# Attention on one core: one transpose per group of maxima, the way through DRAM, and two steps moved between engines

## The reference

```
x = x + alpha * attention(gamma * rmsnorm(x) + beta)
rmsnorm(x) = x * rsqrt(mean(x * x) + 1e-6)
attention: 16 heads of width 16;
  softmax(0.25 * q k^T) v over 512 keys, then @ W_o^T
```

## Time and profile before

| | us |
|---|---|
| median of 3 runs | 1261.8 |
| lowest, highest | 1261.4, 1264.4 |
| the profiled execution's own time | 1264.4 |
| its span, first to last instruction | 1262.6 |

### The profile page before, as it was taken

One profiled execution on the slowest core, in us unless ns is written; L12 is line 12 of the kernel. 1 busy time (PEld: TensorE's weight loads), 2 busy tenths in 40 slices (PEclk: granted clock), 3 DMA queues, 4 the chain that ended last, 5 costly groups with the idle time before them and its releaser, 6 DMA issues. The chain is left out here.

```text
span 1262.6 us, 16655 instructions
## 1 busy us (share of the span) xinstructions
PE 1096.2 (87%) x5282; PEld 654.8 (52%) x5282; DVE 777.3 (62%) x1318; ACT 674.9 (53%) x882; POOL 143.0 (11%) x173
## 2 busy tenths in 40 slices
PE   4879999993578999999999998988828999999994
PEld 3657777772334334343434343432217777777772
DVE  3756776666167777778776878767016555555453
ACT  4453333332306667777777777666424355554445
POOL 0000000001212122232323223021100000000000
PEclk8889999996657999999999999989658999999997
DMA  9522222240342344353435353521030000000000
GB/s 313 224 76 76 76 75 75 76 113 0 120 81 102 84 135 102 95 139 89 131 75 147 64 172 64 169 64 28 12 122 1 2 17 17 17 13 4 17 17 33
DMA packets 54047, 102.09 MB, mean 81 GB/s; under 512 B 8560, under 2 KB 19312, under 8 KB 52976
## 3 DMA queue, kind: packets, MB, share of 16 engines
q1 hardware_dynamic: 51104, 98.86, 27.0%
q10 hardware_dynamic: 2896, 2.64, 0.9%
HBM read 65.02 MB, written 31.72 MB: 77 GB/s over the span
## 5 line engine op out<-in xcount | busy, mean ns | idle before, releaser
L1056 DVE TENSOR_REDUCE mx<-mx_ps 128x1 f32<-128x512 f32 x512 | 329.9, 683 | 129.8 <-PE mx_ps L1131 129.5
L1131 PE MATMUL mx_ps<-kring,qring 48*128 48x512 f32 x512 | 220.1, 490 | 29.5 <-DVE mx L1056 22.6
L1180 PE MATMUL st_ps<-qring,kring 50*128 50x512 f32 x512 | 197.7, 468 | 13.3 <-ACT shared L988 9.6
L1180 PEld LDWEIGHTS st_ps<-qring,kring 50*128 50x128 f32 x512 | 82.9, 195 | 173.0 <-issue 117.0
L988 ACT ACTIVATE pbuf<-st_ps 128x1024 f32<-128x1024 f32 x128 | 129.5, 1022 | 52.3 <-PE st_ps L1180 50.6
L988 ACT ACTIVATE shared<-st_ps 128x1024 f32<-128x1024 f32 x128 | 128.3, 1019 | 37.3 <-PE st_ps L1180 36.5
L1131 PEld LDWEIGHTS mx_ps<-kring,qring 48*128 48x128 f32 x512 | 91.7, 195 | 79.1 <-DVE mx L1056 71.2
L1346 ACT ACTIVATE p_hi<-shared 128x512 fp32r<-128x512 f32 x64 | 40.4, 631 | 93.6 <-DVE shared L1416 93.6
L1420 DVE TENSOR_TENSOR p_lo<-shared,p_hi 128x512 fp32r<-128x512 f32 x64 | 44.3, 693 | 59.2 <-ACT p_hi L1346 59.2
L477 DVE SCALAR_TENSOR_TENSOR h<-val_ps,r,gelu 128x1024 f32<-128x1024 f32 x32 | 41.1, 1284 | 62.4 <-PE val_ps L561 62.4
L1170 PE MATMUL av_ps<-pbuf,vaug 128*17 128x512 f32 x512 | 73.8, 655 | 3.0 <-ACT oaug L916 2.9
(11 more groups left out here) (217 smaller groups left out, 2116.6 us busy)
## 6 DMA issues: line engine op xcount, KB each, us to landing
chunk<-in_gen_w SPq DMA_DIRECT2D x8, 2048.0 KB, 7.8
qring<-q_parts SPq DMA_DIRECT2D x64, 192.0 KB, 3.6
kring<-k_parts SPq DMA_DIRECT2D x64, 192.0 KB, 4.7
q_parts<-stage SPq DMA_DIRECT2D x16, 512.0 KB, 2.8
k_parts<-stage SPq DMA_DIRECT2D x16, 512.0 KB, 2.7
xres<-in_xT SPq DMA_DIRECT2D x8, 512.0 KB, 10.4
shared<-in_x SPq DMA_DIRECT2D x8, 512.0 KB, 9.8
q_parts<-stage SPq DMA_DIRECT2D x16, 256.0 KB, 3.0
```

Source lines behind the costliest of these rows:

```text
L1056: nc.vector.tensor_reduce(mx[h // GH % 2][:, col:col + 1], mx_ps[qt % 2][:], AX, ALU.max).then_inc(S["mx_free"], 1)
L1131: nc.tensor.matmul(mx_ps[qt % 2][:], qring[r:r + QROWS, h // GH, h % GH // 2, qt * P:(qt + 1) * P], kring[r:r + QROWS, h // GH, h % GH // ...
L1180: ins = nc.tensor.matmul(st_ps[half][:, kt % 2], kring[r:r + SROWS, g, i % GH // 2, kt * P:(kt + 1) * P], qring[r:r + SROWS, g, i % GH // ...
```

## The change

`turn_max` makes one transpose of 128x32, each 32x32 block in its own 32 partitions; `split_max` works on 128x32; `store_max` writes both parts to a new DRAM tensor `maxima` (two DMAs, pieces of 128 B) one slot earlier in SyncE's order (slots 1, 5, 9, 13), and `load_max` in slots 2, 6, 10, 14 waits for these and reads the rows into `qring` (two DMAs). VectorE's gamma product is gone: GpSimd multiplies x by rn at the end of slot 15, and ScalarE's activation that adds beta multiplies by gamma as its scale. The rounding copy is made in two halves, and both low parts are made by GpSimd. (The two hunks that only name semaphores and pass `max_dram` on are left out.)

```diff
--- before.py
+++ after.py
@@ -107,12 +107,13 @@
         ko_dram = nc.dram_tensor("k_parts", [NB, NH, QROWS, L], F32, kind="Internal").ap()
         gen_dram = nc.dram_tensor("generated", [2, NB, P, 256], F32, kind="Internal").ap()
         den_dram = nc.dram_tensor("denominators", [NB, NH, L], F32, kind="Internal").ap()
+        max_dram = nc.dram_tensor("maxima", [NB, NG, MPARTS, BLK, P // BLK, BLK], F32, kind="Internal").ap()
 
...
@@ -665,8 +666,8 @@
         oaug = [sb(ctx, f"oaug{i}", [P, L]) for i in range(2)]
         opk = sb(ctx, "opk", [P, KD, L])
         mx = [sb(ctx, f"mx{i}", [P, BLK]) for i in range(2)]
-        mT = sb(ctx, "mT", [BLK, P])
-        mparts = sb(ctx, "mparts", [GH * KT, MPARTS, P], F32R)
+        mT = sb(ctx, "mT", [P, BLK])
+        mparts = sb(ctx, "mparts", [P, MPARTS, BLK], F32R)
 
         st_ps = [pb(ctx, f"st_ps{i}", [P, 2, L]) for i in range(2)]
         mx_ps = [pb(ctx, f"mx_ps{i}", [P, L]) for i in range(2)]
@@ -768,10 +769,17 @@
 
                 wait(sp, "m_lo", NG * b + g + 1)
                 for part in range(MPARTS):
-                    for s in range(2):
-                        row, src = s * HALF + QROWS + part, s * (GH // 2) * KT
-                        sp.dma_start(qring[row:row + 1, g].bitcast(F32),
-                                     mparts[src:src + GH // 2 * KT, part, :].bitcast(F32)).then_inc(mrow[g], 16)
+                    sp.dma_start(max_dram[bass.ds(b, 1), g, part].rearrange("a r n q -> (a n) r q"),
+                                 mparts[:, part].bitcast(F32)).then_inc(S["max_out"], 16)
+
+            def load_max(b, g):
+
+                wait(sp, "max_out", 16 * MPARTS * (NG * b + g + 1))
+                rows = max_dram[bass.ds(b, 1), g].rearrange("a m (s r) n q -> (a m) s (r n q)", r=GH // 2 * KT)
+                for s in range(2):
+                    row = s * HALF + QROWS
+                    sp.dma_start(qring[row:row + MPARTS, g].rearrange("m c q -> m (c q)").bitcast(F32), rows[:, s]) \
+                        .then_inc(mrow[g], 16)
 
             def store_parts(p, m):
 
@@ -815,8 +823,10 @@
                         load_ring(b, 3)
                     if i == 0 and has_f:
                         store_heads(f, 2)
+                    if i in (1, 5, 9) and has_b:
+                        store_max(b, (i + 3) // 4)
                     if i in (2, 6, 10) and has_b:
-                        store_max(b, (i + 2) // 4)
+                        load_max(b, (i + 2) // 4)
                     if 2 <= i < 6 and has_p:
                         store_parts(p, i - 2)
                     if i == 3 and has_f:
@@ -833,8 +843,10 @@
                         load_ring(p, 2)
                     if i == 11 and has_b:
                         store_heads(b, 1)
+                    if i == 13 and has_p:
+                        store_max(p, 0)
                     if i == 14 and has_p:
-                        store_max(p, 0)
+                        load_max(p, 0)
                 if isinstance(j, int) and j == NB + 1:
 
                     sp.wait_ge(S["av_step"], 4 * (NG * NB - 1))
@@ -850,22 +862,20 @@
 
             def split_max(G, b, g):
 
-                if not (isinstance(G, int) and G == 0):
-
-                    pb_, pg = (b, g - 1) if g else (b - 1, NG - 1)
-                    pool.wait_ge(mrow[pg], 32 * MPARTS * (pb_ + 1))
-                wait_apart(pool, "mT", P // BLK * (G + 1), (S["mx_zeroed"], 2))
-                nc.gpsimd.tensor_copy(mparts[:, 0], mT[0:GH * KT, :]).then_inc(S["m_hi"], 1)
+                wait_apart(pool, "max_out", 16 * MPARTS * G, (S["mx_zeroed"], 2))
+                wait_apart(pool, "mT", G + 1, (S["mx_zeroed"], 2))
+                nc.gpsimd.tensor_copy(mparts[:, 0], mT[:]).then_inc(S["m_hi"], 1)
                 wait_apart(pool, "m_hi", G + 1, (S["mx_zeroed"], 2))
-                sub(mparts[:, 1], mT[0:GH * KT, :], mparts[:, 0].bitcast(F32)).then_inc(S["m_lo"], 1)
+                sub(mparts[:, 1], mT[:], mparts[:, 0].bitcast(F32)).then_inc(S["m_lo"], 1)
 
             for j, has_a, has_p, has_b, has_f in iterations(pool):
                 a, p, b, f = j + 1, j, j - 1, j - 2
                 for i in range(NH):
                     if i == 0 and has_p:
 
-                        wait(pool, "h_hi", p + 1)
-                        sub(m_lo[:, 0], hf[:, 0], m_hi[:, 0].bitcast(F32)).then_inc(S["h_lo"], 1)
+                        for k in range(KD):
+                            wait(pool, "h_hi", KD * p + k + 1)
+                            sub(m_lo[:, k], hf[:, k], m_hi[:, k].bitcast(F32)).then_inc(S["h_lo"], 1)
                     if isinstance(j, int) and j == 1 and i == 0:
                         pool.wait_ge(S["setup"], 3)
                     if i < KT and has_b:
@@ -899,6 +909,14 @@
                     if has_max(i, has_p, has_b) and split_group(i) is not None:
                         mb, h = head_of(j, i)
                         split_max(NG * mb + split_group(i), mb, split_group(i))
+                    if i == NH - 1 and has_a:
+
+                        wait_apart(pool, "rn", a + 1, (S["mx_zeroed"], 2))
+                        if has_f:
+                            wait_apart(pool, "addF", f + 1, (S["mx_zeroed"], 2))
+                        for k in range(KD):
+                            nc.gpsimd.tensor_tensor(hf[:, k], x_of(a, k), rn[:], ALU.mult).then_inc(S["t"], 1)
+
 
         @block.scalar
         def _(act):
@@ -941,6 +959,7 @@
                         for k in range(KD):
                             wait(act, "t", KD * p + k + 1)
                             nc.scalar.activation(hf[:, k], hf[:, k], ACT.Identity,
+                                                 scale=cv[:, C_GA, k, bass.ds(p, 1)],
                                                  bias=cv[:, C_BA, k, bass.ds(p, 1)]).then_inc(S["h"], 1)
                     if 2 <= i < 6 and has_p:
                         m = i - 2
@@ -995,9 +1014,10 @@
                         wait_apart(act, "lnd", f + 1, (S["raw_hi"], 3))
                         nc.scalar.activation(hf[:], hf[:], ACT.Exp, scale=-1.0).then_inc(S["rcp"], 1)
                     if i == 0 and has_p:
-                        wait(act, "h", KD * (p + 1))
-
-                        copy(m_hi[:], hf[:]).then_inc(S["h_hi"], 1)
+                        for k in range(KD):
+                            wait(act, "h", KD * p + k + 1)
+
+                            copy(m_hi[:, k], hf[:, k]).then_inc(S["h_hi"], 1)
                     if i == 1 and has_a:
 
                         wait(act, "l1u_ps", 2 * a)
@@ -1039,10 +1059,8 @@
 
                 wait(dve, "mx_free", 16 * (G + 1))
                 wait(dve, "m_lo", G)
-                wait(dve, "mT", P // BLK * G)
-                for n in range(P // BLK):
-                    nc.vector.transpose(mT[:, n * BLK:(n + 1) * BLK], mx[g % 2][n * BLK:(n + 1) * BLK, :]) \
-                        .then_inc(S["mT"], 1)
+                wait(dve, "mT", G)
+                nc.vector.transpose(mT[:], mx[g % 2][:]).then_inc(S["mT"], 1)
 
             for j, has_a, has_p, has_b, has_f in iterations(dve):
                 a, p, b, f = j + 1, j, j - 1, j - 2
@@ -1059,10 +1077,6 @@
 
                     early = 1 if i in (1, 2, 10) else 2
                     take_maxima(range(early))
-                    if i == 1 and has_p:
-                        wait(dve, "h_hi", p + 1)
-                        nc.vector.tensor_tensor(m_lo[:, 1], hf[:, 1], m_hi[:, 1].bitcast(F32), ALU.subtract) \
-                            .then_inc(S["h_lo1"], 1)
                     if 2 <= i < 6 and has_p:
                         m = i - 2
 
@@ -1091,16 +1105,6 @@
 
                         normalise_heads(nc.vector, dve, f)
                         low_heads(nc.vector, dve, f)
-                    if i == NH - 1 and has_a:
-
-                        wait(dve, "rn", a + 1)
-                        if has_f:
-                            wait(dve, "addF", f + 1)
-                        for k in range(KD):
-                            nc.vector.scalar_tensor_tensor(out=hf[:, k], in0=x_of(a, k),
-                                                           scalar=cv[:, C_GA, k, bass.ds(a, 1)], in1=rn[:],
-                                                           op0=ALU.mult, op1=ALU.mult).then_inc(S["t"], 1)
-
         @block.tensor
         def _(pe):
             free = []
@@ -1152,7 +1156,7 @@
                         if h % GH == 0 or (isinstance(j, int) and j == 0 and i == NH - LEAD):
                             pe.wait_ge(ring[mg], 64 * (mb + 1))
                     if has_b and i % GH == 0:
-                        pe.wait_ge(mrow[i // GH], 32 * MPARTS * (b + 1))
+                        pe.wait_ge(mrow[i // GH], 32 * (b + 1))
 
                     has_av = (has_b and i >= GH) or (has_f and i < GH)
 
@@ -1190,8 +1194,7 @@
                         m = i - 1
                         if not (isinstance(j, int) and j == 0):
```

(11 more changed lines are left out.)

## The result

| | before | changed |
|---|---|---|
| median us (4 runs each) | 1263.1 | 1247.5 |
| lowest, highest | 1261.4, 1266.1 | 1244.6, 1251.3 |
| span of the profiled execution | 1262.6 | 1243.6 |

The ratio is 0.9884, 95% interval [0.9853, 0.9914]: 11 to 19 us faster, 14.6 in the best estimate, where I forecast 6.5. The time is inside the range of 1247 to 1263, but by half a microsecond only, and more than twice the gain came, so the sum has to be taken apart. The ratios leave out slow runs (over 1.5% above the fastest of the same kernel) and are not quotients of the medians, from which they lie up to 0.5% (e2). So medians say which way it went, and traces, one execution each, say where.

The account below looks back on a forecast made before the run. TensorE's instruction stream was taken to set the pace, busy 57.3 of 61.5 us. Terms 4.2 + 2.2 - 1.4 + 1.5 = 6.5 us gained, so 1261.8 - 6.5 = 1255.3 us; range 1247 to 1263.

Parts of the forecast that it names:

- First batch: Attention stage's first batch, where no other work covers the new path: 1.4 us lost, bounds 1.0 and 1.8.
- Second batch's turn: Turn with ScalarE and GpSimd idle beforehand: q product 2.2 us earlier, between 0.7 and 3.3.
- Mid-stage path: Turns of six batches, ScalarE's copy to q product: 3.36 us instead of 4.05; 4.2 us gained, bounds 0 and 8.9.
- the rival with 1.77 us: Both GpSimd subtractions at the turn take 1.77 us, mid-stage gives 0, about 1260 us; 18%.
- No new wait: Signs: mid-stage bias never waits for GpSimd, q product waits for GpSimd's m_lo, no score waits for loads of maxima.
- the rival of late rows: Maxima come late through DRAM, TensorE stands at slot 0, about 1272 us; 12%.
- step 1: the clock at the turn: Rival: shorter waits keep TensorE's clock up at about five turns, 6.5 us more gained, 1248.8 us; 15%.
- step 2: the queue, "0": SyncE's DMAs of maxima, two out and two in instead of four: no wait for the rows, 0 us.
- step 3: the parts as a sum: Gains of moves and transposes, counted separately, added: 4.2 + 2.2 - 1.4 + 1.5 = 6.5 us.
- the transposes: Fewer transposes outside the turns: 0.7 us gained in the first batch, 0.8 in slot 8, together 1.5.
- the moves: Gamma products and low parts taken off VectorE: 4.2 us gained at mid-stage turns, 2.2 at the second batch's.

Follow-up runs that it names:

- e2: Changed kernel with the second half's low part back on VectorE and the rounding copy whole: 1244.9 us, ratio 0.9828 to the kernel before.
- e5: Kernel before the change with six unread matmuls filling TensorE's wait at each turn: 1259.1 us, ratio 0.9960.
- e8: e4 with three unread 32x32 transposes per group put back on VectorE: 1253.5 us, ratio 0.9936 to the kernel before.
- e14: e4 with three unread DMA stores in SyncE's queue ahead of the ring's loads: 1253.3 us, ratio 0.9935 to the kernel before.
- e4: Kernel before the change with one transpose per group and the maxima through DRAM alone: 1239.7 us, ratio 0.9837.
- e3: Kernel before the change with the engine moves alone (gamma, low parts, halved copy), four transposes and direct stores kept: 1252.3 us, ratio 0.9933.
- e10: Changed kernel run again unchanged, on another call: 1246.5 us, ratio 0.9862 to the kernel before.
- e9: e4 with slot 1's value matmuls issued after the second half of the scores: 1260.9 us, ratio 0.9968 to the kernel before.
- e1: Changed kernel with the gamma products back on VectorE and no scale in ScalarE's activation: 1243.0 us, ratio 0.9868 to the kernel before.
- e11: e4 with the denominators issued ahead of the ring's loads in SyncE's queue: 1272.7 us, ratio 1.0075 to the kernel before.
- e13: Kernel before the change with the denominators issued ahead of the ring's loads in SyncE's queue: 1295.5 us, ratio 1.023.

## Why the prediction was right or wrong

**Right, by its own steps.** *First batch*: 1.4 us lost. From rn ready to the product it takes 6.54 us, 5.19 before, so 1.35. (My own terms add up to 6.74, which less 5.16 is 1.6; the 1.4 written down was closer by luck.) Each hand-over shows:

```profile
320.72 0.63 ACT L951 ACTIVATE rn<-rn 128x512 f32<-128x512 f32 x1
321.42 2.48 POOL L918 TENSOR_TENSOR hf<-xres,rn 128x512 f32<-128x512 f32 x2 [3.65 <-ACT rn L951]
...
323.94 0.81 ACT L961 ACTIVATE hf<-hf,cv 128x512 f32<-128x512 f32 x1 [0.41 <-POOL hf L918]
...
324.66 1.13 ACT L934 ACTIVATE m_hi<-hf 128x512 fp32r<-128x512 f32 x2
...
325.35 2.48 POOL L861 TENSOR_TENSOR m_lo<-hf,m_hi 128x512 fp32r<-128x512 f32 x2 [1.44 <-ACT m_hi L934]
...
327.89 0.80 PE L1122 MATMUL st_ps<-m_hi,wq_lo 128*128 128x512 f32 x1 [7.93 <-POOL m_lo L861]
```

*Second batch's turn*: 2.2 forecast. From rn's last instruction to the product it took 14.25 us (371.88 to 386.13), now 12.17 (371.40 to 383.57), so 2.1. The 2.16 between products (57.84 us, now 55.68) is another sum: it also holds the wait behind the first transposes, which fell from 0.71 to 0.25 us where I forecast 0.7 gained, and 0.4 us lost ahead of that. *Mid-stage path*: 3.36 from copy to product forecast, 3.28 here. With the 0.21 us transpose the undisturbed turn went from 9.79 to 8.94 us, 0.85 for my 0.7. Both subtractions of GpSimd take 1.25 to 1.29 us, so the rival with 1.77 us falls. *No new wait*: in mid-stage the bias doesn't wait for GpSimd, the wait at the product names GpSimd's `m_lo`, and no score waits for the rows of maxima. The two loads follow the two stores by 2.9 us, as in the tightest place, where slot 0's score at 573.72 waits only for ScalarE:

```profile
564.66 1.44 SPq L772 DMA_DIRECT2D maxima<-mparts  x2
567.52 0.71 SPq L781 DMA_DIRECT2D qring<-maxima  x2
```

So the rival of late rows falls. The Trainium skill (DMA: Bandwidth & Descriptors, Specifications) has transfers under 512 B done as a read-modify-write; twice as many packets under 512 B as before (16112, 8560) left no wait in this trace that could be laid to it. The 2.0 us per DMA that I took from that page stand there for DMAs issued by GpSimd; these are SyncE's.

**Wrong, step 1: the clock at the turn.** I counted 1.3 us at some five turns as a rival at 15%, "against it: by my own path a wait of some 1.4 us stays". The wait stayed, 1.31 us, and the fall at the products went all the same: 1.58 us in all five batches, 0.80 less on average, some 4 us over the stage (the second product still takes 2.83 us, and in this trace the eighth 2.80). e5 shows that in the kernel before the idle time made the fall, and e8, with a wait of up to 1.5 us again, falls in some batches. The earlier trace rows itself had a wait of 1.48 us with no fall behind it, where other turns fell, so the argument "a wait stays" could not decide it. What tips it between 1.31 and 1.48 us stays open. With this rival in it my sum was 1248.8, at 15%, and the median is 1247.5; that this is so close is luck, as slots 9 to 11 (step 2) made up for the price. The rival's price was too high as well (0.8, not 1.3, averaged over turns that fell and turns that didn't).

**Wrong, step 2: the queue, "0".** I asked only whether the new DMAs could come late, so the term had a loss as its far end and no gain. What I did not ask was what stands behind the four row stores that go: the ring's loads, and behind these the denominators that ScalarE waits for in slot 8. Slots 9 to 11 gave 0.60 us a batch, 3 to 4 us in all. e14 puts 0.7 us of that delay back into e4 by itself, and the waits come back, with 0.7 to 1% of the time: the term is not nothing. How much of the changed kernel's own 0.60 us is the queue's is not shown, since e3 gained 0.81 us there without touching the queue, and e8 lost half or more of e4's gain there with the new queue in place. Rows of the trace of before would have told: ScalarE waited 6.5 us in five batches for the denominators.

**Wrong, step 3: the parts as a sum.** I let the transposes work only in slot 8 and in the first batch (1.5 us, where the moves got 4.2 + 2.2). At the turn they stand on the same path as the low part: alone they shorten it more than the moves do (e4). The sum of both parts counted apart, 8 and 17 to 20 us, is nearly twice the 15 measured together.

Added up by measured stretches: -1.35 + 2.16 up to the second product, 0.69 for the third, 5 x 2.08 for the five of the table, 2.76 for the end: 14.7 us. The end of the stage was not followed up by an experiment, nor was the spread of slots 9 to 11 in one kernel (8.8 to 12.6 us in the changed one). Of the 0.34 us a batch in slots 2 to 8, 0.24 belong to the transposes part: e3, which leaves it out, takes 27.06 there, and I had looked at slot 8 alone. In the last of the five batches the turn took 10.39 us, in the four others 8.89 to 8.96: the clock fell in it (0.64 granted from 763 to 774 us), and the eighth product, which the table leaves out, took 2.80 us. In the same kernel run again (e10) it took 1.56. What made this fall is open. In the changed kernel's worst batch the wait for the denominators is 1.87 us, and the clock is down in the whole stretch, 0.76 against 1.00 in the next batch; that the wait brings the clock down there is not shown:

```profile
541.30:553.90 12.60, 10.46 (x44) 3.92 (x44) 7.28 (x13) 8.61 (x9) 6.33 (x5) 0.76 0.29 63
609.90:619.30 9.40, 8.46 (x46) 3.35 (x43) 7.37 (x13) 8.01 (x9) 5.22 (x5) 1.00 0.39 77
```

## What to carry to other kernels

Removing four small things from one in-order queue moves all that follows: before putting "0" beside a queue, name the next transfer behind the removed ones and who waits for it. Two edits that shorten the same path are not summed: work out the path with each alone. And put work of TensorE that isn't urgent ahead of its waits: idle time there costs itself and can cost the low clock of what follows (e9).

## What the runs showed of the hardware

- VectorE's and GpSimd's subtractions of 128x512 lengthen each other by their order: started together, 0.69 and 1.78 us (e4); with VectorE 0.5 us behind, 1.35 and 1.29; GpSimd alone 1.28.
- A transpose of 128x32 in 32x32 blocks takes 212 ns, about as long as one block of 32x32 (200 ns; four take 0.89 us).
- ScalarE's Identity on 128x512 takes 819 ns with a scale per partition and 723 without (e1):

```profile
L961 ACT ACTIVATE hf<-hf,cv 128x512 f32<-128x512 f32 x14 | 10.8, 819 | 1.8 <-POOL hf L918 1.8
```

```profile
L953 ACT ACTIVATE hf<-hf,cv 128x512 f32<-128x512 f32 x14 | 9.7, 723 | 6.7 <-DVE hf L1105 6.3
```

- ScalarE's logarithm starts on average 8.3 us behind the issue of the 256 KB spread of the denominators in the kernel before (six batches, 7.2 to 8.7), 8.2 in e14, 7.9 in e3 (7.0 to 9.2), and 7.2 in e4 (6.8 to 7.9, two of them without a wait). Over all kernels but e11 and e13: where the ring's first load is issued 3.2 us ahead of the denominators, 7.2 (21 batches, 6.8 to 7.8); where it is 2.4 to 2.9 us ahead, 8.0 (51 batches, 6.7 to 9.2). With the ring's loads behind them 7.0 in e11 and 7.1 in e13. So loads issued shortly ahead delay the landing by about a microsecond, with a wide spread.
